# Gating and row scatter moved into the main loop of a two-layer transformer kernel, expert regions in place of packed slots, and heads restacked through DRAM

## The reference

```python
h = _L0_tok_ref(...)                          # state-space kernel: makes the 8 x 256 x 256 tokens from x
h = layernorm(h + _L0_attn_ref(h, ...))       # causal attention, 8 heads of 32, a geometric bias
h = layernorm(h + _L0_ffn_ref(h, ...))        # attention with 32 heads of 8, then a fixed-split expert FFN (8 experts, gelu)
h = layernorm(h + _L1_attn_ref(h, ...))       # gated linear attention, 4 heads
h = layernorm(h + _L1_ffn_ref(h, ...))        # gated mixture, top 2 of 8 experts, hidden 1024, relu

# _L1_ffn_ref
gate_scores = softmax(x @ Wg + bg)                       # 2048 tokens x 8 experts
h = relu(einsum('btc,ech->bteh', x, W1) + b1)            # W1: 8 x 256 x 1024
expert_out = einsum('bteh,ehc->btec', h, W2) + b2        # W2: 8 x 1024 x 256
topk_scores, topk_idx = top_k(gate_scores, 2)
out = sum(take(expert_out, topk_idx) * softmax(topk_scores))
```

## Time and profile before

| | us |
|---|---|
| median of 3 runs | 1401.38 |
| the profiled execution, its own time | 1397.64 |
| span of its trace | 1395.8 |
| TensorE busy | 1067.5 (76%) |
| VectorE busy | 734.2 (53%) |
| ScalarE busy | 492.1 (35%) |
| GpSimd busy | 153.5 (11%) |

### The profile page before, as it was taken

The page is one execution under the profiler, slowest core; times in us unless marked ns, Lnnn a source line. Parts: engine busy times, 40 slices in busy tenths (PEclk is TensorE's granted clock), DMA queues, the critical chain, the costliest instruction groups (busy, mean ns, idle before and its releaser), DMA issues. The chain is left out here.

```text
span 1395.8 us, 23281 instructions
## 1 busy us (share of the span) xinstructions
PE 1067.5 (76%) x8552; PEld 784.0 (56%) x8552; DVE 734.2 (53%) x1910; ACT 492.1 (35%) x988; POOL 153.5 (11%) x210
## 2 busy tenths in 40 slices
PE   1239978897989896997878988875503999999980
PEld 1225745444665465663446635734502999999980
DVE  7972445664536756548666463445140444444446
ACT  2111423454554443544535652520000333333322
POOL 4950000000000000000000000000044111111110
PEclk7558987888999899999989996985555999999995
DMA  9221020000121000120000300200982111111105
GB/s 236 60 72 31 1 76 15 1 16 1 31 84 31 16 2 1 46 69 31 1 1 17 105 25 1 76 0 0 327 321 78 31 40 39 39 39 32 39 32 180
DMA packets 62445, 78.29 MB, mean 56 GB/s; under 512 B 14640, under 2 KB 52288, under 8 KB 62208
## 3 DMA queue, kind: packets, MB, share of 16 engines
q1 hardware_dynamic: 57088, 62.11, 14.1%
q0 software_dynamic: 4672, 14.57, 3.3%
q10 hardware_dynamic: 576, 0.13, 0.0%
HBM read 55.94 MB, written 20.85 MB: 55 GB/s over the span
## 5 line engine op out<-in xcount | busy, mean ns | idle before, releaser
L1499 DVE TENSOR_REDUCE mx<-scores_ps 128x4 f32<-128x1024 f32 (+1 forms) x160 | 186.9, 1168 | 129.6 <-PE scores_ps L1007 78.9
L1348 ACT ACTIVATE pt<-turned_ps 128x1024 f32<-128x1024 f32 (+1 forms) x160 | 157.9, 987 | 148.2 <-PE turned_ps L1029 104.3
L1956 PEld LDWEIGHTS x_ps<-x_xtT,x_w1s 128*128 128x128 f32 x1248 | 147.2, 194 | 3.5 <-ACT x_xtT L1991 1.6
L1956 PE MATMUL x_ps<-x_xtT,x_w1s 128*128 128x128 f32 x1248 | 147.7, 277 | 1.0 <-ACT x_xtT L1991 1.0
L1968 PE MATMUL x_ps<-x_w,x_hT 128*128 x624 | 141.0, 379 | 0.0
L1968 PEld LDWEIGHTS x_ps<-x_w,x_hT 128*128 128x128 f32 x624 | 115.6, 190 | 14.1
L2103 DVE COPY x_w1s<-x_w 128x2048 f32 x39 | 55.3, 1421 | 81.2 <-PE x_ps L1956 64.7
L1019 PE MATMUL turned_ps<-q,k 32*128 32x256 f32 x512 | 71.5, 353 | 29.5 <-DVE mx L1499 21.6
L957 POOL COPY vpad<-v 128x64 f32<-128x64 f32 x64 | 13.9, 248 | 720.6 <-PE ps L1068 590.5
L1019 PEld LDWEIGHTS turned_ps<-q,k 32*128 32x128 f32 x512 | 44.2, 203 | 85.0 <-issue 45.9
L1991 ACT COPY x_xtT<-x_ps 128x256 f32<-128x256 f32 x39 | 14.5, 372 | 218.2 <-PE x_ps L1938 218.2
(11 more groups left out here) (419 smaller groups left out, 1984.9 us busy)
## 6 DMA issues: line engine op xcount, KB each, us to landing
wexp<-in_L_ffn_w SPq DMA_DIRECT2D x16, 1024.0 KB, 5.2
x_w<-in_L_ffn_W SPq DMA_DIRECT2D x16, 1024.0 KB, 13.2
x_slots<-s_zero POOLq DMA_DIRECT2D x1, 5070.0 KB, 33.6
x_xt<-x_slots SPq DMA_DIRECT2D x39, 130.0 KB, 2.1
ha<-h SPq DMA_DIRECT2D x16, 256.0 KB, 3.0
x_pair<-y_rows SPq DMA_DIRECT2D x4, 1024.0 KB, 9.5
x<-hb SPq DMA_DIRECT2D x8, 256.0 KB, 2.5
x_acc<-x SPq DMA_DIRECT2D x4, 512.0 KB, 6.1
```

Source lines behind the costliest of these rows:

```text
L1348: sc.activation(pt[v.index // 2 % (PT_RING // 2)][:, :, 0:wide], turned_ps[:, :, 0:wide], ACT.Exp)\
L1499: v.tensor_reduce(mx[:, u.group % 2, 0:blocks, u.n:u.n + 2].rearrange("p b n -> p n b"), scores_ps[:, :, 0:blocks * (P if u.causal else T) ...
L1956: last = mm(ps[2 * (i % 2) + f // KH][:, f % KH * P:(f % KH + 1) * P], w1s[:, i % 2, c, f * P:(f + 1) * P], xtT[:, i % 2, c, :], start=c = ...
```

## The change

Six parts.

1. `x_slots` holds a region of 2048 rows for each expert and 896 rows more: 17280 rows, 18.0 MB. The zeros are no longer written by one DMA of GpSimd but by five DMAs that ScalarE issues, after its four copies of `xT` and before it copies the factors. ScalarE waits at the end of stage one until they have landed.
2. `spreading` stays for pair 0 alone. For pairs 1 to 3 SyncE stores `nat` to a DRAM tensor `heads` (4 DMAs) and loads it in the stacked form (32 DMAs of 64 KB for each sequence). The stage Y2s goes for these pairs, and Y2 becomes Y2d, 4 slots shorter.
3. Y1b has four more slots: transposes of the pair's tokens, scores, choice of experts, counts. VectorE keeps running totals per expert. GpSimd scatters the pair's rows (8 indirect DMAs) as soon as its places are known. `x3` and its stores and loads go.
4. The expert weights are loaded from the end of the main loop on, when pair 3 has signalled `h3`, with a semaphore for each expert. For this the buffers of the mixture are laid where those of the main loop were.
5. A small table (`tables`) gives each tile the number of its expert and its first row. GpSimd loads the tiles by indirect DMAs, three ahead.
6. In the mixture's block b1 and b2 are loaded first; the wait for all weights becomes one per expert.

```diff
-            pool.dma_start(xs.rearrange("(p r) d -> p r d", p=P),
-                           zero[:, :].unsqueeze(1).to_broadcast([P, rows, xs.shape[1]])).then_inc(zeroed, 16)
...
             # ScalarE, behind its copies of xT
+            act.wait_ge(constants, 3)
+            rows = xs.shape[0] // P // 5
+            for i in range(5):
+                act.dma_start(xs.rearrange("(p i r) d -> i p r d", p=P, i=5)[i],
+                              zero[:, :].unsqueeze(1).to_broadcast([P, rows, xs.shape[1]])).then_inc(zeroed, 16)
             act.wait_ge(columns, 4)
             for k in range(6):
                 act.wait_ge(squares, k + 1)
...
+            act.wait_ge(zeroed, 16 * 5)
...
-                (1.75, 1.7, 0, False, "p2_1"), (0, 3, 0, True, ""), (0, 1.8, 0, True, "")],
+                (1.75, 1.7, 0, False, "p2_1"), (0, 3, 0, True, ""), (0, 1.8, 0, True, ""),
+                (.95, .7, .6, True, "gx_t0 gx_t1"), (1.7, 1.2, .6, True, "gs"), (0, 4.5, .5, True, ""),
+                (.4, 5, 0, True, "gc")],
...
+        def load_heads(p, bb):
+            reached[p, bb] += 1
+            if reached[p, bb] < 2:
+                return
+            sp.wait_ge(sg("nat_out"), 64 * p)
+            sp.wait_ge(sg("st_full"), half_free(p, bb))
+            for w, (dst, which) in enumerate(((q1, "q"), (k1, "k"))):
+                for h, part in enumerate(("_hi", "_lo")):
+                    rows = heads[p, w, h].rearrange("t (a r d) n -> r d (t a) n", a=4, r=4)
+                    for quarter in cn.PARTS[which + part]:
+                        for r in range(4):
+                            at = 32 * r + 8 * quarter
+                            sp.dma_start(dst[at:at + 8, bb, :, :].bitcast(fp32), rows[r, :, :, bb * T:(bb + 1) * T])\
+                                .then_inc(sg(f"heads_in{bb}"), 16)
...
         def y1b(p):
-            yield from pause(22)
-            sp.wait_ge(sg("h3"), p + 1)
-            for bb in range(2):
-                sp.dma_start(x3[p + PAIRS * bb]...
+            yield from pause(23)
+            if p == PAIRS - 1:
+                sp.wait_ge(sg("h3"), PAIRS)
+                mixture.load_experts(sp)
+            yield from pause(4)
...
+        def scatter(p):
+            pool.wait_ge(sg("slots"), p + 1)
+            for tb in range(NTB):
+                for k in range(2):
+                    g.indirect_dma_start(out=xs[:, :],
+                                         out_offset=bass.IndirectOffsetOnAxis(gt.slot[:, p, k, tb:tb + 1], 0),
+                                         in_=gt.hbx[p % 3][:, tb, :], in_offset=None).then_inc(sg("scattered"), 16)
...
+        plan.weave(x_stream(), stream("a"), stream("b"))
+        pool.wait_ge(sg("scattered"), 16 * 8 * PAIRS)
...
             # the mixture's block, SyncE
+            sp.dma_start(b1r[:, :], io["L1_ffn_b1"]...).then_inc(sg("b1_in"), 16)
+            sp.dma_start(b2b[:, :, :], io["L1_ffn_b2"].partition_broadcast(P)).then_inc(sg("b2_in"), 16)
...
+                g.indirect_dma_start(out=xt[:, i % XR, :], out_offset=None, in_=xs[:, :],
+                                     in_offset=bass.IndirectOffsetOnAxis(mx.source[:, i:i + 1], 0))
...
-            pe.wait_ge(sg("b1"), 1)
+            pe.wait_ge(sg("b1_in"), 16)
+            tr(ps[7][:, 0:E * FT], b1r[:, :], ident[0:E * FT, 0:E * FT]).then_inc(sg("b1_full"), 1)
             rows_t(0)
             pe.wait_ge(sg("te"), 1)
-            pe.wait_ge(sg("w_in"), 16 * (2 * E + 1))
+            pe.wait_ge(sg("b1"), 1)
```

More of the change, by code:

```diff
@@ L647, in needs @@
         after("Y1b", 2, 22, "Y1b", 3, 21)
+        after("Y1b", 2, 26, "Y1b", 3, 23)
         return needs
@@ L755, in done, with main_loop @@
         return self.freed[self.at[name, p]]
-def main_loop(nc, ctx, whole, io, h0, x3, ident, weights, consts):
+def main_loop(nc, ctx, whole, io, h0, xs, heads, ident, weights, consts, gates, claim):
     plan = Plan()
@@ L896, in a_stream @@
                     continue
-                if stage == "Y2":
+                if stage in ("Y2", "Y2d"):
                     yield from pause(6)
                     next_ha(stage, p, "xn_t1")
+                if stage == "Y2d":
+                    yield from pause(6)
+                    store_natural(p)
+                    for bb in range(2):
+                        load_heads(p, bb)
+                    yield
+                    continue
                 yield from pause(len(plan.STAGES[stage]) - (6 if stage == "Y2" else 0))
@@ L961, in _, with x_stream, stream @@
             ends.append(unit.index + 8)
+        def x_stream():
+            for s in range(len(plan.slots)):
+                us = plan.two(s, 0)
+                if us and not us[0].causal and us[0].n == 0:
+                    pad(us[0])
+                yield
+        def scatter(p):
+            if p == PAIRS - 1:
+                mixture.number_tiles(g)
+            pool.wait_ge(sg("slots"), p + 1)
[4 more added lines that the diff above has]
+                                         in_=gt.hbx[p % 3][:, tb, :], in_offset=None).then_inc(sg("scattered"), 16)
+        def stream(side):
+            for stage, p in plan.ORDER[side]:
+                for k in range(len(plan.STAGES[stage])):
+                    if stage == "Y1b" and k == 26:
+                        scatter(p)
+                    yield
+        plan.weave(x_stream(), stream("a"), stream("b"))
+        pool.wait_ge(sg("scattered"), 16 * 8 * PAIRS)
     @block.tensor
@@ L1178, in y2 @@
                 yield
-            evicted("n3", p)
-            yield from spreading(p, 0)
+            if p == 0:
+                evicted("n3", p)
+                yield from spreading(p, 0)
         def spreading(p, bb):
@@ new lines, in expert_mixture @@
+def expert_mixture(nc, ctx, io, mixture, out, ident):
+    mx = mixture
+    E, FT, XR, TILES, GRP = mx.E, mx.FT, mx.XR, mx.TILES, mx.GRP
+    KH, NG = FT // 2, mx.NB // GRP
+    gt, sg, xs, ys = mx.gates, mx.sg, mx.xs, mx.ys
+    ROW, FIRST, SHARE, MORE = gt.ROW, gt.FIRST, gt.SHARE, gt.MORE
+    w1, w2, w1s, xt, xtT, hT, y, pair = mx.w1, mx.w2, mx.w1s, mx.xt, mx.xtT, mx.hT, mx.y, mx.pair
+    b1r, b1c, b2b, te, tef, row, rs = mx.b1r, mx.b1c, mx.b2b, mx.te, mx.tef, mx.row, mx.rs
+    other, share, own, rowf, shift, stats, mv = mx.other, mx.share, mx.own, mx.rowf, mx.shift, mx.stats, mx.mv
```

524 lines of the change are left out of this document (283 added, 241 removed).

## The result

The changed kernel takes 1424.63 us (median of 4 runs, 1422.4 to 1425.51), the kernel before 1401.66 us (median of 4, 1400.92 to 1402.03). The ratio is 1.0148, with a 95% interval of 1.0119 to 1.0177: it is slower by 1.5%, where 1389 us, 0.9% faster, was forecast. The profiled execution of after took 1425.31 us, its span is 1423.4 us, against 1397.64 and 1395.8 before.

The account below looks back on a forecast made before the run. VectorE bounds stage one, TensorE X1 and tiles; the tail is a chain. 1397.6 - 45.5 + 39 - 15 + 9 = 1385.1, with 3.7 for the median 1389 us; range to 1407, low end taking in 1348; forecast's own 1374 to 1405.

Parts of the forecast that it names:

- X1 part: Main loop, 221.9 to 840.9 us: spreading slots leave (32 us), gates of pairs 0 and 1 enter (17): net -15 us.
- Cover is there, by 3 us: Pair 3's heads through DRAM take 23 us; the six slots before its X1 give 26 us, so no wait.
- rival D: Pair 3's heads come late: loads issued each 0.9 us, not 0.5, its first sequence waits 10 us, 1399 us; chance 0.05.
- 12 us of waits on VectorE's blocks: X1 part: TensorE waits some 3 us for each of 4 gate blocks on VectorE, within the gates' 17 us.
- Stage one: Start of kernel, 0 to 96.8 us: ScalarE held by five zeroing DMAs, so VectorE starts at 61.7, not 22.7: +39 us.
- Rival B: Stage one: ScalarE is not held by the zeroing DMAs, the 39 us go, total 1350 us; chance 0.17.
- Tail: End of main loop, 840.9 to 977.3 us: pair 2's gate joins the chain with pair 3's last products: +9 us.
- Prologue: From T, the main loop's last norm's end, to the first tile's first transpose: 92.9 to 47.4 us, -45.5.
- Tiles: The mixture's tiles, 1070.2 us to the end: stay bound by TensorE, no term in the sum.
- bound of -38: Prologue's smaller gain if scatters and loads share the rate badly: 2 x 4 MB at 244, not 380 GB/s, add 7.5 us.
- Rival C: Gates cost the main loop more than spreading did: X1 part +4 instead of -15, total 1413 us; chance 0.12.
- the prediction's 1400 rows: Stage one's rule for held issues: a DMA issue ends when about 1400 rows are still ahead in its queue.

Follow-up runs that it names:

- fourth experiment: Changed kernel with the last projection of pair 3's queries and keys 12 score slots ahead of the first that reads the heads, not 6: 1406.98 us, 1.0031 of before.
- sixth experiment: Changed kernel with the heads of pairs 1 to 3 spread by TensorE again, gates and all else as changed: 1446.76 us, 1.0315 of before.
- ninth: Changed kernel with one small gate step on VectorE done 17 times over at both of its places: 1440.16 us, 1.0285 of before.
- third experiment: Changed kernel with two of the five zeroing DMAs on ScalarE, the rest zeroed by SyncE in 27 pieces in the main loop: 1385.76 us, one run.
- second experiment: Changed kernel with the same five zeroing DMAs issued by GpSimd at the start instead of ScalarE: 1434.68 us, 1.0227 of before.
- fifth: Changed kernel with each of the 32 head loads going into 32 partitions instead of 8, same bytes, results wrong: 1407.4 us, one run.
- tenth experiment: Changed kernel with b1 and b2 loaded ahead of the expert weights and experts 4 to 7 issued after the barrier: 1415.31 us, 1.0087 of before.
- first: Changed kernel with the zeroing issued by SyncE in 27 pieces in the main loop, not by ScalarE in stage one: 1389.1 us, 0.990 of before.
- seventh: Changed kernel with pair 3's projections 12 slots early, plus the gate's VectorE steps in five planner slots instead of two: 1400.46 us, 0.9979 of before.
- eighth experiment: Changed kernel with TensorE's products for the gate's scores done four times over: 1460.17 us, 1.0391 of before.
- eleventh: Changed kernel with late SyncE zeroing, early pair 3 projections, five gate slots, early b1 and b2, two experts ahead of the barrier: 1344.21 us, 0.9559 of before.
- twelfth: Changed kernel with late SyncE zeroing, early pair 3 projections, early b1 and b2, two experts ahead of the barrier, gate in two slots: 1347.45 us, 0.9601 of before.

## Why the prediction was wrong

Against the profiled executions the forecast was 1385.1 and the result 1425.3, 40.2 us apart. By its steps:

- *X1 part, -15 forecast, +12.6 measured: the step that failed.* "Cover is there, by 3 us" was wrong, and it turned the sign of this term: the heads of pair 3 came 19.6 us late. The chain took 39.2 us (723.99 to 763.18) and not 23, and the six slots covered 19.6 (to 743.6) and not 26. The stores took 7.0 us up to the first load (3.1 and 3.9), 4.5 forecast. The loads took the rest. I gave each 0.5 us for its issue, 16 in all, and 2.5 to the last to land; the issues took 18.6 in all, and the last one landed 13.5 us after it, at the rate of its transfers. I took issue and landing from rows of other shapes, and never asked at what rate a DMA into 8 partitions moves. The slots' 4.3 us were a mean over the part; near its end they come each 3.3. This was rival D, which had a chance of 0.05 and a wait of 10 us from slower issues; its place was right, its price half, and its reason was not the one, as the issues took 0.58 us each. The fourth experiment shows the step: without the wait the kernel is at 1406.98. That is just inside the whole range, which ended at 1407, and above the 1374 to 1405 that I gave the forecast itself; its ratio of 1.0031 (0.9997 to 1.0065) is no gain. So this step alone is not all of the error: it holds 17.7 of the 40.2 us, and the next 9.9.
- *The same part without the wait:* 611.8 us, -5.1 in place of -15. The spreading was worth 40.1 us in the loop (forecast 32) and the gates cost 36.1 (forecast 17), each known to some 10 us. I priced a gate's work on TensorE at 2.7 us; the sixth experiment has 3.8 at the full clock and 6.2 for a gate that fell mostly on the half one. The 12 us of waits on VectorE's blocks were too many: at their own length TensorE idled 4.4 us more (sixth experiment), and only a longer block is paid in full (ninth). What I had no term for is the lower granted clock of everything else, which goes with 21.7 us and whose cause is open. The loop gained 4.0 us by the trade of the two, no more.
- *Stage one, +39 forecast, +44.5 measured:* the mechanism was right, and so was the rule for it. Five DMAs held ScalarE for 54.85 us, 47.3 forecast, as 14.2 MB moved at 259 GB/s and not at 300 (50.8 to 52.5 us in other profiles with the same five). Two held it for 10.5 us (third experiment). Rival B, no hold, is out. The rule of the Trainium skill beside it ("DMA: Bandwidth & Descriptors", section "Issuing engines are not separate DMA queues"), that initiating a DMA is usually small relative to the DMA itself, does not hold here: 54.85 us of issuing are not small beside transfers that land 35.7 us (median) after their issue began.
- *Tail, +9 forecast, +11.2 measured:* the gate of pair 2 stands in the chain as thought.
- *Prologue, -45.5 forecast, -40.6 measured:* the barrier fell at T + 39 as forecast, and b1 was what the first tile waited for. It came at T + 52 and not T + 46.5, since its own issue was held for 4.5 us behind the weights, and the scatters' and the first fetches' rows moved beside them at 368 GB/s, not 380.
- *Tiles:* +0.2, as forecast.
- *Two readings that do not come out, and changed no term of the sum.* Rival B's "no DMA as large as 3456 rows is in the trace" overlooks the kernel before's own zeroing, 4992 rows in one DMA, which GpSimd issued in 2.18 us; the second experiment shows that GpSimd's queue takes more at once. And 8 MB at 244 in place of 380 GB/s add 11.7 us to the prologue, not 7.5, so the bound of -38 was too near.

Rival C, which stood for "slower", would have decided at an X1 part of 615 us or more. The part took 629.5, but by the heads' wait; without it 611.8 is below that point. The gates did cost what C feared and more, and the spreading gave back what C denied.

## What to carry over

A DMA's time is its shape before it is its bytes: before a transfer is put under a cover of a few slots, find a row of a DMA with the same number of partitions, and count from the first issue to the last landing at that rate. An engine that issues more than its queue takes stops until the rest fits; SyncE, ScalarE and GpSimd all did so here. So give long zeroing or weight loads in small pieces to an engine that nobody waits for, and put small urgent loads ahead of large ones. And a barrier counts every engine's issues: what the other side doesn't need at once belongs behind it.

## What the runs showed of the hardware

- GpSimd's queue took 13824 rows of about 1 KB at once and then held it for 61 us. ScalarE was held by the second of two DMAs of 3456 rows, which fits the prediction's 1400 rows.
- 32 DMAs of 64 KB into 8 partitions each moved at about 70 GB/s, the same bytes into 32 partitions at 140, both with 1 KB rows; the stores of the same data moved at 380.
- The granted clock makes stretches of equal instructions differ from profile to profile. X1 of pair 1, with no gate in it, took 167.7 to 167.8 us in five profiles (that of after at 0.93, the third, fifth, ninth and tenth experiment) and 174.1 to 174.8 in seven others (the first, second, fourth, seventh, eighth, eleventh and twelfth, at 0.89 to 0.90); the sixth has another order there. All changed kernels have 0.87 to 0.90 over the main loop, and the kernel before 0.91. Whether the gates cause that was not isolated; it stays open, and with it 21.7 of the gates' 36.1 us.
- A gate's 16 passes for the scores took 1.95 us at a granted clock of 1.00 and 3.55 to 3.58 at 0.50. In a row of 64 of them the clock fell from 1.00 to 0.50 while TensorE was busy all the time (eighth experiment, at 570 and at 803 us).
